# Attention rows searched in halves throughout, with the differences from TensorE and the threshold on VectorE

## The reference

```python
x = x + 0.5 * ffn(layernorm(x))        # job b
x = x + attn(layernorm(x))             # 16 heads of 16, keys 512
x = x + 0.5 * ffn(layernorm(x))        # job a

# attn, for every (batch, head, query) row of 512 scores
scores = q @ k.T / sqrt(D)
thresh = top_k(scores, U)[0][..., -1:]       # U = 31
scores = where(scores < thresh, -inf, scores)
context = softmax(scores) @ v

# ffn: 16 experts, a gate that keeps the experts with a positive logit, or the best two if there are none
logits = normalize(x) @ normalize(sim) - sigmoid(gates)
rw = softmax(where(mask > 0, relu(logits), -inf))
q, k, v = (sum over experts of rw * (x @ w_e) for w in (q, k, v))
attn = softmax(causal(q @ k.T / 8)) @ v
out = sum over experts of (attn * rw_e) @ o_e
```

## Time and profile before

| | us |
|---|---|
| median of 3 runs | 4321.31 (4321.08 to 4321.35) |
| profiled execution | 4318.63 |
| its span in the trace | 4316.8 |

### The profile page before, as it was taken

One profiled execution on the slowest core, in us unless ns is written; L12 is line 12 of the kernel. 1 busy time (PEld: TensorE's weight loads), 2 busy tenths in 40 slices (PEclk: granted clock), 3 DMA queues, 4 the chain that ended last, 5 costly groups with the idle time before them and its releaser, 6 DMA issues.

```text
span 4316.8 us, 91531 instructions
## 1 busy us (share of the span) xinstructions
PE 3792.6 (88%) x29004; PEld 3111.9 (72%) x29004; DVE 4052.2 (94%) x14267; ACT 3484.2 (81%) x8005; POOL 3624.1 (84%) x4170
## 2 busy tenths in 40 slices
PE   6777889899998989899898989989998999987777
PEld 5556777777777777777777777777777777765566
DVE  3389999999999999999999999999999999999992
ACT  2377889888888988888898888888888888887772
POOL 1467999999999999999999999999999999976650
PEclk8888999999999999999999999999999999998888
DMA  3111122121212212122212122122222122210112
GB/s 101 47 33 33 53 55 59 55 57 53 60 55 56 57 53 58 55 59 55 59 53 59 55 56 57 54 58 55 59 55 58 52 60 55 55 42 26 27 31 54
DMA packets 243925, 230.33 MB, mean 53 GB/s; under 512 B 27123, under 2 KB 176628, under 8 KB 243316
## 3 DMA queue, kind: packets, MB, share of 16 engines
q1 hardware_dynamic: 243444, 224.49, 19.2%
HBM read 214.98 MB, written 9.44 MB: 52 GB/s over the span
## 4 chain that ended last, share of the span: by engine, by line
DVE 87%; PE 7%; ACT 3%; POOL 1%; DMA 1%; issue 1%; SPq 0%; ACTq 0%; POOLq 0%; DVEq 0%
DVE M L895 14%; DVE HL L897 11%; DVE HL L925 7%; DVE HL L919 7%; DVE HL L911 7%; DVE HL L915 6%; DVE M L927 6%; DVE M L923 6%; DVE M L909 5%; DVE HL L917 5%; DVE M L913 5%; DVE HL L921 5%; PE pQ L596 3%; DVE nm_a L876 1%; DVE nm_b L876 1%
## 5 line engine op out<-in xcount | busy, mean ns | idle before, releaser
L596 PE MATMUL pQ<-wf_sb,HS 128*128 128x192 f32 x8192 | 1483.3, 336 | 118.5 <-POOL HS L364 95.0
L596 PEld LDWEIGHTS pQ<-wf_sb,HS 128*128 128x128 f32 x8192 | 1379.8, 196 | 166.2 <-issue 139.5
L798 ACT ACTIVATE S<-S,M 128x512 f32<-128x512 f32 x1024 | 766.3, 748 | 8.9 <-DVE M L895 6.0
L804 ACT ACTIVATE S<-S,lift 128x512 f32<-128x512 f32 x1024 | 754.0, 736 | 3.0 <-POOL lift L962 2.9
L364 POOL TENSOR_TENSOR HS<-hT_a,RB 128x1024 f32<-128x1024 f32 x244 | 578.1, 2369 | 0.1
L364 POOL TENSOR_TENSOR HS<-hT_b,RB 128x1024 f32<-128x1024 f32 x240 | 567.6, 2365 | 4.2 <-PE pQ L596 2.2
L614 PE MATMUL pST<-ident,S 128*128 128x128 f32 x4096 | 506.8, 279 | 16.8 <-ACT S L784 12.8
L971 POOL TENSOR_TENSOR S<-HL 128x512 f32<-128x512 f32 x384 | 493.3, 1285 | 30.1
L794 ACT COPY PTs<-pST 128x1024 f32<-128x1024 f32 x512 | 495.0, 1021 | 28.5 <-PE pST L614 28.1
L969 POOL TENSOR_TENSOR HL<-S,HL 128x512 f32<-128x512 f32 x384 | 491.9, 1281 | 29.3 <-ACT HL L788 29.2
L614 PEld LDWEIGHTS pST<-ident,S 128*128 128x128 f32 x4096 | 473.1, 145 | 32.7 <-ACT S L784 14.1
(11 more groups left out here) (255 smaller groups left out, 8367.8 us busy)
## 6 DMA issues: line engine op xcount, KB each, us to landing
RB<-rows_b SPq DMA_DIRECT2D x384, 256.0 KB, 3.5
RB<-rows_a SPq DMA_DIRECT2D x384, 256.0 KB, 3.4
x_b<-in_x SPq DMA_DIRECT2D x64, 128.0 KB, 3.3
out_y<-y SPq DMA_DIRECT2D x64, 128.0 KB, 2.0
wf_sb<-in_wf SPq DMA_DIRECT2D x4, 768.0 KB, 6.9
rows_b<-rwT SPq DMA_DIRECT2D x64, 8.0 KB, 1.3
wof_sb<-in_wof SPq DMA_DIRECT2D x1, 1024.0 KB, 6.8
rows_a<-rwT SPq DMA_DIRECT2D x64, 8.0 KB, 1.3
```

Of the source, the lines that this page charges most:

```text
L596: mm = nc.tensor.matmul(pQ[:, 0:QKV], HS[:, m % 2, e, i, :], wf_sb[:, i, at:at + QKV], start=k + e + i == 0, stop=(k, e, i) == (3, 3, 1))
L798: nc.scalar.activation(S[:, r, :], S[:, r, :], ACT.Prelu, bias=M8[:, r, TH:TH + 1], scale=-1.0, alpha=1.0 / STEEP).then_inc(s_cut, 1)
L804: nc.scalar.activation(S[:, r, :], S[:, r, :], ACT.Exp, bias=lift[:, r:r + 1], scale=-STEEP).then_inc(s_gap, 1)
```

## The change: what it does

Every pair is now halved; the whole-row branch is gone. TensorE makes the difference first (`differences`, step SD: 128x256 for each head, into the first half of the head's bank), ScalarE takes one Relu of it (ED, d+), and TensorE then overwrites the bank with both halves' scores (SC, which waits for that Relu through `s_rd`). EV is one copy for every pair. GpSimd has two steps a pair: hi = second + d+, lo = first - d+. The threshold is no longer the 31st value but half of `edge`, the sum of the 31st and the 32nd; `edge` (step EDGE) and `lift` are both made on VectorE, each once a quad, and CUT waits for EDGE. `HL` has 12 places instead of 16. In the gate, `top` falls into `top`, `pair` and `repl` in slots of their own, `gate` loses an instruction, and `gate_exp` waits for `guard` (VectorE) instead of `gate` (GpSimd). Most slots move, many to quarters.

```diff
 # tables of slots (many other steps of the two feed-forward jobs move by 0.25 to 3 slots)
-RINGH = 16
+RINGH = 12
-"top": 83, "gate": 87, "gate_exp": 88, "gate_em": 89, "gate_sum": 90,                        # job a
+"top": 84.5, "pair": 85.5, "repl": 86.5, "gate": 87.75, "gate_exp": 87.75, "gate_em": 88.75, "gate_sum": 89,
-AT["SC"] = series(2, 4, QUADS, {0: -4, 1: 1, 2: 7, 3: 10})
+AT["SC"] = series(2.3, 4, QUADS, {0: -4, 1: 1, 2: 7, 3: 10})
+AT["SD"] = series(1.5, 4, QUADS, {0: -4.6, 1: -1, 2: 6.3, 3: 9.2})
+AT["ED"] = series(1.6, 4, QUADS, {0: -4.3, 1: -.5, 2: 6.6, 3: 9.4})
-AT["SPLIT"] = series(5, 2, PAIRS, ...)
-AT["TOP"] = series(6, 2, PAIRS, ...)
-AT["CUT"] = series(10, 1, UNITS)
-AT["LIFT"] = series(11, 4, QUADS)
-AT["EXPS"] = series(12, 1, UNITS)
+AT["SPLIT"] = series(5.75, 2, PAIRS, ...)
+AT["TOP"] = series(7, 2, PAIRS, ...)
+AT["CUT"] = series(11.5, 1, UNITS)
+AT["EDGE"] = series(10.5, 4, QUADS)
+AT["LIFT"] = series(12.5, 4, QUADS)
+AT["EXPS"] = series(13.25, 1, UNITS)
 # TensorE
+            def differences(n):
+                for h in range(HG):
+                    nc.tensor.matmul(pST[:, h, 0:HALVES], QT[...], KK[r:r + 32, g // 2, 1, :], ...).then_inc(s_dif, 1)
             def scores(n):
                 for h in range(HG):
+                    pe.wait_ge(s_rd, 4 * n + h // 2 * 2 + 2)
                     nc.tensor.matmul(pST[:, h, :], QT[...],
-                                     KK[r:r + 32, g // 2, 0::2, :] if (2 * n + h // 2) % GANG in FULL else KK[r:r + 32, g // 2, 1:3, :],
+                                     KK[r:r + 32, g // 2, 0::2, :],
 # ScalarE, EV: now for every pair of rows
-                        if u // 2 % GANG in FULL:
-                            nc.scalar.copy(S[:, r:r + 2, :], pST[:, h:h + 2, :]).then_inc(s_ev, 2)
-                            continue
-                        nc.scalar.copy(S[:, r:r + 2, HALVES:T], pST[:, h:h + 2, HALVES:T])
-                        nc.scalar.activation(HL[:, e:e + 2, 0:HALVES], pST[:, h:h + 2, 0:HALVES], ACT.Relu)
-                        nc.scalar.activation(HL[:, e:e + 2, HIL:HIL + HALVES], pST[:, h:h + 2, 0:HALVES], ACT.Relu, scale=-1.0
-                                             ).then_inc(s_ev, 2)
+                        nc.scalar.copy(S[:, r:r + 2, :], pST[:, h:h + 2, :]).then_inc(s_ev, 2)
+                if (n := WHEN["ED"].get(s)) is not None:
+                    for h in range(0, HG, 2):
+                        act.wait_ge(s_dif, u + 2)
+                        wait(act, s_tk, searched(u + 1 - RINGH))
+                        nc.scalar.activation(HL[:, e:e + 2, HIL:HIL + HALVES], pST[:, h:h + 2, 0:HALVES], ACT.Relu
+                                             ).then_inc(s_rd, 2)
 # ScalarE, CUT and EXPS: the threshold is now half of edge; the exponent's scale is halved
-                    wait(act, s_tk, searched(u))
-                    nc.scalar.activation(S[:, r, :], S[:, r, :], ACT.Prelu, bias=M8[:, r, TH:TH + 1], scale=-1.0, ...
+                    act.wait_ge(s_edge, u // 4 + 1)
+                    nc.scalar.activation(S[:, r, :], S[:, r, :], ACT.Prelu, bias=edge[:, r:r + 1], scale=-2.0, ...
 # ScalarE, gate_exp
-                    act.wait_ge(q["gate"], 4 * t + 4)
+                    act.wait_ge(q["guard"], t + 1)
 # VectorE: the branch of whole rows (for i, k in WHOLE) is gone; every pair goes through ORDER
+                if (n := WHEN["EDGE"].get(s)) is not None:
+                    wait(dve, s_tk, searched(4 * n + 3))
+                    nc.vector.tensor_tensor(edge[:, r:r + 4], M8[:, r:r + 4, TH], M8[:, r:r + 4, TH + 1], ALU.add
+                                            ).then_inc(s_edge, 1)
+                if (n := WHEN["LIFT"].get(s)) is not None:
+                    dve.wait_ge(s_edge, n + 1)
+                    nc.vector.scalar_tensor_tensor(lift[:, r:r + 4], edge[:, r:r + 4], 0.5, M8[:, r:r + 4, 0],
+                                                   ALU.mult, ALU.subtract).then_inc(s_lift, 1)
 # GpSimd
-                if (n := WHEN["LIFT"].get(s)) is not None:
-                    wait(pool, s_tk, searched(4 * n + 3))
-                    nc.gpsimd.tensor_tensor(lift[:, r:r + 4], M8[:, r:r + 4, TH], M8[:, r:r + 4, 0], ALU.subtract
-                                            ).then_inc(s_lift, 1)
-                if (n := WHEN["SPLIT"].get(s)) is not None and n % GANG not in FULL:
+                if (n := WHEN["SPLIT"].get(s)) is not None:
-                    nc.gpsimd.tensor_tensor(hi, second, hi, ALU.add).then_inc(s_hi, 1)
-                    pool.wait_ge(s_hi, HALVED[n])
-                    nc.gpsimd.tensor_tensor(first, hi, lo, ALU.subtract)
-                    nc.gpsimd.tensor_tensor(lo, second, lo, ALU.subtract).then_inc(s_lo, 1)
+                    nc.gpsimd.tensor_tensor(hi, second, lo, ALU.add).then_inc(s_hi, 1)
+                    nc.gpsimd.tensor_tensor(lo, first, lo, ALU.subtract).then_inc(s_lo, 1)
 # gate: the subtraction R - L is gone, three instructions instead of four
-                ns.tensor_tensor(J.fb[:], J.R[:], J.L[:], ALU.subtract).then_inc(g, 1)
-                ns.tensor_scalar(J.fb2[:], J.fb[:], 0.0, J.na[:], ALU.is_lt, ALU.mult).then_inc(g, 1)
+                ns.tensor_scalar(J.fb2[:], J.R[:], 0.1 * -BIG, J.na[:], ALU.is_lt, ALU.mult).then_inc(g, 1)
```

More of the change, by code:

```diff
@@ L1 @@
 from contextlib import ExitStack
-from itertools import accumulate
 import concourse.bass as bass
@@ L57 @@
     "a": {k: v - 2 * TILE for k, v in {
[L58 to L62, removed]
+        "ctx_rec": 65.75, "ctx_norm": 70.75, "ctxT": 72.25, "x": 74, "x_sq": 75.5, "x_rstd": 76.5, "h": 77.5,
@@ new lines @@
+        "hT": 78.5, "h_rinv": 80.75, "lg": 81, "shift": 83, "top": 84.5, "pair": 85.5, "repl": 86.5, "gate": 87.75,
+        "gate_exp": 87.75, "gate_em": 88.75, "gate_sum": 89, "rw": 91.25, "rwT": 92, "rw_st": 92.75, ("rb", 0): 92.75,
+        ("hs", 0): 96.25, ("rb", 1): 96.5, ("pq", 0): 97.25, ("hs", 1): 99, ("pq", 1): 99.5, ("rb", 2): 100,
+        ("rb", 3): 100, ("hs", 2): 100.25, ("pq", 2): 101, ("hs", 3): 102.5, ("pq", 3): 103, "qkv": 103.75,
+        "qkT": 105, "sc": 109, "sc_max": 109.75, "sc_exp": 111, "sc_rec": 112.5, "sc_norm": 112.75, "pT": 114.75,
@@ L63 @@
+        "attT": 116.5, "rb2": 118.25, "mix": 118.25, "y": 119, "out": 123,
     }.items()},
     "b": {k: v - SPAN for k, v in {
[L65 to L68, removed]
@@ L69 @@
[L69 removed]
+        "x_ld": -49.75, "x_sum": -49.5, "x_sq": -48, "x_rstd": -46, "h": -43.5, "hT": -43, "h_rinv": -41, "lg": -41,
+        "shift": -38.75, "top": -38.5, "pair": -37.5, "repl": -36.5, "gate": -34, "gate_exp": -33.25,
+        "gate_em": -32.5, "gate_sum": -32, "rw": -30.75, "rwT": -30.25, "rw_st": -29, ("rb", 0): -26.25,
+        ("rb", 1): -25.25, ("rb", 2): -24.5, ("hs", 0): -24, ("pq", 0): -23, ("hs", 1): -22.25, ("rb", 3): -22,
@@ L129 @@
 RANGE = [(n, "hs", t) for _, n, t in sorted((s, n, t) for n in "ab" for k in range(4) for t, s in enumerate(AT[n, "hs", k]))]
[L132 to L137, removed]
 def passed(u, k):
-    return PASSED[u // 2] + order(u // 2).index((u % 2, k)) + 1 if u >= 0 else 0
+    return u // 2 * len(ORDER) + ORDER.index((u % 2, k)) + 1 if u >= 0 else 0
 def searched(u):
-    return passed(u, order(u // 2)[-1][1])
+    return passed(u, ALL16)
 def place(u):
@@ L209, in build @@
         M8 = sb("M8", P, RING, RANKS)
+        edge = sb("edge", P, RING)
         lift = sb("lift", P, RING)
@@ L348, in layer @@
                 ns.tensor_tensor(J.ep[:], J.eg[:], J.pos[:], ALU.mult).then_inc(q["gate_em"], 1)
-                wait(eng, q["gate"], 4 * t + 4)
+                wait(eng, q["gate"], 3 * t + 3)
                 eng.wait_ge(q["gate_em"], 2 * t + 1)
@@ L618, in slot @@
                     nc.tensor.transpose(pO[:, P:2 * P], cT[:], ident[:]).then_inc(s_ot, 1)
-                if (n := WHEN["SC"].get(s)) is not None:
+                if (n := WHEN["SD"].get(s)) is not None:
+                    wait(pe, s_ev, 4 * n)
+                    wait(pe, s_pe, 4 * (n - 3))
                     if n % PER in (0, 2):
                         pe.wait_ge(s_kd, n // PER * 2 + n % PER // 2 + 1)
-                    wait(pe, s_ev, 4 * n)
-                    wait(pe, s_pe, 4 * (n - 3))
+                    differences(n)
+                if (n := WHEN["SC"].get(s)) is not None:
                     scores(n)
@@ L866, in ffn @@
                     nc.vector.max(J.v8[:, 0:8], J.L[:]).then_inc(q["top"], 1)
+                if (t := tile(J, "pair", s)) is not None:
                     dve.wait_ge(q["top"], t + 1)
@@ L871, in ffn @@
                                             ).then_inc(q["guard"], 1)
+                if (t := tile(J, "repl", s)) is not None:
                     dve.wait_ge(q["pair"], t + 1)
```

76 lines of the change are left out of this document (33 added, 43 removed).

## The result

The changed kernel takes 4336.9 us (median of six runs, 4331.9 to 4341.5), the kernel before 4321.3 (six runs beside them, 4319.3 to 4323.6). The ratio is 1.0037, with a 95% interval of 1.0024 to 1.0050: slower by 0.4%. The forecast was slower by 2.8%.

A forecast was written before the change was run, and what follows sets the result against it. VectorE was taken as the bound, busy 269.5 of 270 us in the middle. 4318.6 - 197 + 64 - 18 = 4168, + 271 = 4439, plus 2.7 for the median: 4442 us, 2.8% slower; range 4215 to 4560.

The forecast's parts named there:

- Whole pairs become halved: VectorE's search: 128 whole pairs at 8.71 us become halved ones at 7.17, saving 197 us.
- The gate's steps spread: VectorE's gate: its instructions, set apart, no longer wait for each other; 0.14 us by 128 tiles, saving 18 us.
- EDGE and LIFT: Two small steps on VectorE, 256 each, at 0.17 and 0.08 us if nothing stands in their way: +64 us.
- the hold-up: On VectorE, two-input EDGE and LIFT wait until the GpSimd instruction under way has ended: +271 us over 512 places.
- 0.53: Assumed mean wait in us of EDGE and LIFT for GpSimd's instruction, taken between 0.32 and 0.76.
- My bounds, 0.32 to 0.76: Mean wait per place in us: 0.32 if only LIFT pays, 0.76 if VectorE always meets GpSimd at work.
- The ends: First and last stretches of the span, 250 us, where moved slots were allowed 10 us either way.
- The break-even of 0.29 us: Mean wait at each of 512 EDGE and LIFT places that eats the gain; below it faster, above it slower.
- The moved slots, SyncE's loads of RB and RB2 among them: Changed issue slots, said to cost nothing as long as the middle belongs to VectorE.
- The rival of TensorE's bound: With small waits, TensorE at 265 us against VectorE's 260 per middle stretch sets the time: 4246 us; chance 0.08.
- The rival of slipping through: EDGE and LIFT on VectorE, only four elements, are not held up by GpSimd: 4171 us, 3.4% faster; chance 0.16.

The follow-up runs named there:

- experiment 1: The changed kernel with `edge` and `lift` both made one-input reductions on VectorE: 4309.4 us, 0.9971 of the kernel before.
- experiment 7: The changed kernel, two-input steps kept, with only job a's RB2 load issued earlier (slot 114.5 instead of 118.25): 4374.7 us, 1.0119 of the kernel before.
- experiment 6: The changed kernel with both one-input reductions and job a's RB2 load at slot 114.5 instead of 118.25: 4148.6 us, 0.9599 of the kernel before.

## Why the prediction was right in direction and too high in size

- **Whole pairs become halved: right.** From start to start over the whole trace the searches took some 3868 us before and 3673 after: -195, forecast -197.
- **The gate's steps spread: right.** Some 70 to 50 us by the same count: -19, forecast -18.
- **EDGE and LIFT: right in mechanism, too high in size.** The forecast had +64 for the steps themselves and, on top of that, +271 for the hold-up, 335. Start to start they take 263. Against the same steps with one input (experiment 1), 227 of them are hold-up, 0.44 us at each of 512 places, which leaves 36 for the steps.
- **The step that failed is the addition: the time GpSimd still had to run, 0.53 us at each of 512 places, was charged in full on top of what a step costs alone.** That time was forecast well: when a step starts, GpSimd's large instruction has 0.52 us left on average of all 512 places, 267 us for 271. But a held step ends 0.02 us after GpSimd's instruction instead of running its own 0.16 us after it, and the next instruction starts some 0.06 us before that end. So the 357 held steps cost, start to start, 0.04 us less than the time GpSimd had left; the other 155 cost 0.07 us each. Together that is 263 us, where the forecast added 64 to its 271 and got 335. The hold-up above a step's own cost is therefore 0.44 us and not 0.52.
- **That 0.53 came out was luck.** A moment that knows nothing of GpSimd would have met 0.63 us by the large instructions of this trace (an estimate: their lengths squared over twice the time), about the forecast's 0.64. I went down to 0.53 because EDGE might come while GpSimd stands still. It was the other way round: 216 of the 256 EDGEs started under a large instruction, with 0.59 us to run as the mean of all, and 141 of the LIFTs, with 0.45. GpSimd is busy in the middle about as assumed (233.0 of 270 us, 86%, for 84%), and it was met idle 84 times of 512, no more often than its idle time says. But the moment isn't a random one: the slots repeat, and with them the phase. By the slot of one load alone the mean hold-up of `lift` went from 0.39 us (the change, against experiment 1) to 0.62 (experiment 7). My bounds, 0.32 to 0.76, hold both; shares of time alone don't say where between them a schedule will lie.
- **The ends: sized at nothing, they were worth -25.** VectorE's idle time over the whole trace fell from 265 to 240 us. The first search starts at 171.8 us instead of 177.3, the ninth pair at 245.2 instead of 266.5; in the first stretch VectorE is busy 124.8 us instead of 105.2. The beginning gives 20 of the 25: in the last 270 us of each program, counted from its own end, VectorE is busy 181.6 us instead of 178.4. I had allowed 10.
- The sum: -72 on EDGE and LIFT (-4 on the time left, -68 on what was added to it), -25 at the ends, +1 from the other terms, makes 4439 - 96 = 4343 for a profiled execution, and it took 4341.5.
- **The break-even of 0.29 us** was argued with 64 us for the steps. With the measured terms it is (195 + 19 + 25 - 36) / 512 = 0.40 us, and 0.44 measured, hence a kernel only 0.4% slower.
- **"The moved slots, SyncE's loads of RB and RB2 among them, cost nothing as long as the middle belongs to VectorE": right for this kernel, and the reason that it hid a second bound.** Experiment 7 shows that RB2's late load cost it next to nothing, 1 and 6 that it costs 161 us as soon as the hold-up is gone.
- **The rival of TensorE's bound** (4246) had too small a price: by it experiment 1 would have been at about 4246, and was at 4309. I had counted only TensorE's own work, 256 to 265 us a stretch. The difference matmuls were well bracketed (138 to 274 us forecast, 185.4 measured), but its waits, and the matmuls at the lower clock behind each, were not in it. With these waits gone it is at 4149 (experiment 6).
- **The rival of slipping through** fell for GpSimd's large instructions (in this trace, every step that came more than 0.15 us before the end of one waited for it), and holds for its small ones.

## What to carry to other kernels

A small operation between two large ones of a full VectorE is priced by how many tensors it reads and by what GpSimd does then, not by its size. The wait replaces the operation's own time rather than adding to it. Look for a form with one input (a reduction over neighbouring places) before anything else. When a change removes work from the bound and the time stays, look for a second bound that was built in the same change; here each of the two cures alone was worth -28 and +38 us, and both together -188. A slot of a load is also a place in a queue: what it stands behind decides when it is issued.

## What was unexpected in the hardware

- GpSimd's instructions of 256 elements a row and more held a two-input instruction of VectorE (until 0.02 us after their end in the median, 0.08 at most, of the 317 steps that came more than 0.15 us before it). Its steps of one or 16 elements a row did not: the 71 steps that met only these took 0.16 us, as beside an idle GpSimd; one `lift` took 0.14 us under a power of 0.56 us.
- A held step can be passed by the next instruction of GpSimd: a `lift` of experiment 7 came 1.09 us before the end of RB2's product, was held through the HS and the product behind it as well, and took 3.98 us. Another there took 3.58.
- After a wait of 1.92 us in experiment 1 TensorE's granted clock was 0.53 for 3.4 us, and eight float32 matmuls took 3.56 us instead of 1.89. There the clock cost almost as much again as the wait.
- In a program with a fixed order the hold-up depends on the phase of the two engines: 538 to 768 ns for the same instruction, by slots that were moved or steps that were changed elsewhere.
